# Layer 1 of a two-layer graph kernel: from group by group to batches of four groups

## The reference

```python
h = (x @ W).reshape(n, NHEAD, OUT_FEATS)            # 4 heads of 64
h_l = (a_l * h).sum(-1); h_r = (a_r * h).sum(-1)
e = h_l[row] + h_r[col]
e = jnp.where(e > 0, e, ALPHA * e)
m = jax.ops.segment_max(e, row, num_segments=n)
ex = jnp.exp(e - m[row])
denom = jax.ops.segment_sum(ex, row, num_segments=n)
att = ex / (denom[row] + 1e-16)
out = jax.ops.segment_sum(att[:, :, None] * h[col], row, num_segments=n)
```

## Time and profile before

| | us |
|---|---|
| median of 3 runs (lowest, highest) | 2514.63 (2512.04, 2518.51) |
| the profiled execution | 2514.38 |
| its span in the profile | 2512.6 |
| busy PE, DVE, ACT, POOL | 2155.4, 1961.2, 1689.9, 1587.8 |

### The profile page before, as it was taken

How to read it: one execution, slowest core, us unless ns; L and a number is a source line. 1 busy time by engine, 2 the same in 40 slices (tenths; PEclk the granted TensorE clock), 3 DMA queues, 4 the chain that set the end, 5 groups by cost and what they waited for, 6 DMA issues and landing times.

```text
span 2512.6 us, 62086 instructions
## 1 busy us (share of the span) xinstructions
PE 2155.4 (86%) x14858; PEld 1765.1 (70%) x14859; DVE 1961.2 (78%) x6401; ACT 1689.9 (67%) x6944; POOL 1587.8 (63%) x1700
## 2 busy tenths in 40 slices
PE   0579999999968888888888888869999999999994
PEld 0347777777747777777766776658888888888883
DVE  8983333333338999998989998879999999999998
ACT  2125555555547777777777775558888888888883
POOL 5346777777776565655555563157777777777772
PEclk9999999999989999999999999989999999999997
DMA  7243333333339999989989995123323222223232
GB/s 226 85 175 115 128 126 129 125 129 125 127 124 333 302 306 313 306 301 300 312 290 304 308 310 161 39 74 81 80 78 79 79 78 79 78 79 81 79 78 69
DMA packets 153328, 413.79 MB, mean 165 GB/s; under 512 B 40848, under 2 KB 53045, under 8 KB 153282
## 3 DMA queue, kind: packets, MB, share of 16 engines
q0 software_dynamic: 79360, 301.93, 37.4%
q1 hardware_dynamic: 73922, 111.33, 13.7%
HBM read 328.69 MB, written 84.60 MB: 164 GB/s over the span
## 4 chain that ended last, share of the span: by engine, by line
DVE 36%; issue 20%; DMA 18%; PE 12%; ACT 9%; DVEq 4%; POOL 1%; ACTq 0%; SPq 0%; POOLq 0%
DMA sorted_edges<-arena,idxA 8%; DMA arena<-sorted_edges 8%; DVE gmax L1111 6%; PE ps L1250 4%; ACT arena L617 3%; DVE arena L973 3%; DVE work L1130 2%; ACT arena L608 2%; DVE el L1106 2%; DVE hrmax L1119 2%; DVE sc L987 2%; DVE arena L980 2%; DVE gmax L1083 2%; PE ps L1283 2%; DVEq L286 1%
## 5 line engine op out<-in xcount | busy, mean ns | idle before, releaser
L548 POOL DMA_INDIRECT arena<-node_row,idxB x464 | 454.5, 980 | 209.2 <-issue 103.6
L474 POOL DMA_INDIRECT sorted_edges<-arena,idxA x416 | 410.4, 987 | 148.3 <-issue 147.4
L1361 PE MATMUL ps<-ident_b,arena 128*128 128x128 bf16 x5568 | 390.4, 220 | 53.0 <-DVE gmax L1111 26.8
L944 DVE TENSOR_TENSOR arena<-ps,b_bc 128x512 f32<-128x512 f32 x208 | 143.8, 691 | 354.6 <-PE ps L1250 354.6
L1250 PE MATMUL ps<-w_sb,arena 128*128 128x256 f32 x1664 | 386.9, 386 | 22.1 <-ACT arena L608 18.2
L1361 PEld LDWEIGHTS ps<-ident_b,arena 128*128 128x128 bf16 x5568 | 331.4, 100 | 87.8 <-DVE gmax L1111 31.4
L1250 PEld LDWEIGHTS ps<-w_sb,arena 128*128 128x128 f32 x1664 | 308.3, 190 | 99.8 <-issue 56.2
L494 POOL DMA_INDIRECT work<-node_kvx,idxB x232 | 234.3, 1010 | 165.1 <-issue 52.4
L494 POOL DMA_INDIRECT arena<-node_kvx,idxB x232 | 233.1, 1005 | 166.4 <-issue 53.0
L626 ACT ACTIVATE away<-iota,srcB 128x128 f32<-128x128 f32 x928 | 315.0, 386 | 0.2
L1283 PE MATMUL ps<-arena,work 128*128 128x256 f32 x928 | 252.9, 396 | 58.1 <-issue 52.1
(11 more groups left out here) (168 smaller groups left out, 4909.2 us busy)
## 6 DMA issues: line engine op xcount, KB each, us to landing
arena<-sorted_edges SPq DMA_DIRECT2D x232, 260.0 KB, 5.1
arena<-in_edge_attr SPq DMA_DIRECT2D x25, 512.0 KB, 3.6
node_kvx<-arena SPq DMA_DIRECT2D x24, 384.0 KB, 2.3
arena<-node_row,idxB POOLq DMA_INDIRECT x464, 2.8
sorted_edges<-arena,idxA POOLq DMA_INDIRECT x416, 2.4
sorted_edges<-arena SPq DMA_DIRECT2D x25, 260.0 KB, 2.1
sorted_edges<-arena SPq DMA_DIRECT2D x1, 6240.0 KB, 21.1
arena<-node_kvx,idxB POOLq DMA_INDIRECT x232, 5.2
```

The source lines that it names most:

```text
L474: pool.indirect_dma_start(rec_dram[:, :], bass.IndirectOffsetOnAxis(ap=idxA[:, st.slot(4), c:c + 1], axis=0), recA[:, st.slot(4), c, :], N ...
L548: pool.indirect_dma_start(row1_g[:, st.slot(8), j, :], None, row1_dram[:, :], bass.IndirectOffsetOnAxis(ap=idxB[:, st.slot(8), j:j + 1], a ...
L1361: pe.matmul(bank[:, h * P:(h + 1) * P], parts[:, i:i + 1].to_broadcast([P, P]), ident_b[:, :], start=h == 0 and part == 0, stop=False)
```

## The change

Four consecutive groups make a batch (BG = 4, 58 batches), and the loop is unrolled by 16.

- Spreading h_r: the 12 parts of both chunks are transposed by two matmuls with 12 stationary columns (`trh`), ACT copies them to SBUF (`hrT`), and for each head one matmul of 256 columns with a selector of 12 rows (`sel`) adds the three parts up on every row. The penalty is added by two matmuls of 512 columns. A group's four heads fill two banks, and a second pair of banks is for the next group.
- DVE takes one maximum over 256 numbers for each of 4 heads (1024 per row), the running maxima of a batch by one scan and three small steps backward, so that all groups of a tile in one batch share their maximum, and one rescaling of the running sums per batch in place of ACT's four per group.
- h_l, maxima, e and e - m are handled for the 8 chunks of a batch at once. The exponential is one of 32 numbers.
- DVE multiplies the messages of both chunks; POOL only gathers, and the gathered rows have 16 slots.
- The sums of a group have one PSUM bank, not two.

```diff
+    BG = 4
+    NB = NG // BG
+    ME = BG + 2
+    PARTS = 3 * NH1
...
 def gather1(st):
-    (POOL's product for chunk 1, L536)
+    if st.u % BG == 0:
+        pool.wait_ge(s("idxC_ready"), batch(st).n + 1)
+    if not st.first(16):
+        pool.wait_ge(s("msg1_ready"), st.n - 15)
...
 ACT, layer1(st):
+    g, b = st.u % BG, batch(st)
+    if g == 0:
+        f = b.back(-2)
+        if f.real():
+            indices(f)
+        e = b.back(2)
+        if e.real():
+            r = e.slot(2)
+            act.wait_ge(s("em"), e.n + 1)
+            ...
+            act.activation(ew[:, r, :, :], em[:, r, :, :], ACT.Exp).then_inc(s("exp1"), 1)
+            act.wait_ge(s("mdiff"), e.n + 1)
+            ...
+            act.activation(mscale[:, r, :], mdiff[:, r, :], ACT.Exp).then_inc(s("mscale"), 1)
+    if st.u % 8 == 0:
+        act_tiles[0] = tiles16(ACT_ENGINE, st.k, 0, st.u // 8)
+    if st.real():
+        (hl copy, two aways, one-hot)
+    c = st.back(1)
+    if c.real():
+        (pen, onehT8, hrT)
...
 DVE, layer1(st):
+    c = st.back(8)
+    if c.real():
+        (at the first group of a batch: rescale acc, wait for it)
+        dve.wait_ge(s("agg1_ready"), c.n + 1)
+        dve.tensor_tensor(acc, acc, ps[:, 5, 0:NH1 * HE], ALU.add)
+    if st.real():
+        dve.wait_ge(s("hr_mm"), st.n + 1)
+        dve.reduce_max(gmx[:, b.slot(2), :, 2 + g],
+                       ps[:, bank:bank + 2, :].rearrange("p c (h e) -> p (c h) e", h=2), axis=AX.X)
+    e = b.back(1)
+    if g == 1 and e.real():
+        (ez, el, es, em of 32, each waits for the one before)
+    m = st.back(6)
+    if m.real():
+        (at the first group of a batch: wait for exp1 of the batch)
+        (msg1 of both chunks, 520 per row)
+    if g == BG - 1 and st.real():
+        top(b, st)
...
+def top(b, last):   # each step waits for the one before
+    step(dve.tensor_tensor_scan(mfw, fresh, gmx, -BIG, ALU.add, ALU.max))
+    step(dve.tensor_copy(gmx[:, 1 - r, :, 0], mfw[:, :, ME - 1]))
+    for e in range(ME - 2, 1, -1):
+        step(dve.scalar_tensor_tensor(mfw[:, :, e], mfw[:, :, e + 1], fresh[...], mfw[:, :, e], ALU.add, ALU.max))
+    step(dve.tensor_tensor(zz, mfw[:, :, 1:ME], hmx[:, r, 0, :, :], ALU.add))
+    step(dve.scalar_tensor_tensor(hmx[:, r, 1, :, :], zz, SLOPE, zz, ALU.mult, ALU.max))
+    dve.sem_inc(s("hm_ready"), 1)
+    dve.tensor_tensor(mdiff[:, r, :], hmx[:, r, 1, 0, :], hmx[:, r, 1, 1, :], ALU.subtract)
...
 PE, layer1(st):
+    if st.real():
+        pe.wait_ge(s("oneh1"), n + 1)
+        transposes(r, oneh1[:, r16, 0, :], oneh1[:, r16, 1, :], s("oneh_tr1"))
+        pe.wait_ge(rows_in(r16), rows_base(r16) + 32 * st.turn(16) + 32)
+        (two matmuls into trh)
+    b = st.back(2)
+    if b.real():
+        (penalty 512 and two heads of 256, twice, waits gmax of two groups before)
+    e = batch(b).back(1)
+    if b.u % BG == 0 and e.real():
+        pe.wait_ge(s("onehT1"), BG * e.n + BG)
+        pe.wait_ge(s("hm_ready"), e.n + 1)
+        (8 matmuls, onehT8 stationary, 8 columns each)
+    d = st.back(9)
+    if d.real():
+        pe.wait_ge(s("msg1_ready"), n + 1)
+        pe.wait_ge(s("acc1_done"), n)
+        (two matmuls that sum the messages)
```

More of the change, by code:

```diff
@@ L33 @@
 BIG = 2.0 ** 100
+NEW = 2.0 ** 110
+FAR = 2.0 ** 120
 SLOPE = 0.2
@@ L289, in tiles_of, with tiles16, rows_in, rows_base @@
             return values
+        def tiles16(eng, k, lag, half):
+            _, values = nc.values_load_multi_w_load_instructions(
+                gt_i[0:1, bass.ds(k * 16 + (8 - lag + 8 * half), 8)], engines=(eng,), min_val=0, max_val=NT - 1,
+                skip_runtime_bounds_check_because="the table's values are bounded by the minimum with NT - 1")
+            return values
+        def rows_in(r):
+            if r < 8:
+                return s(f"kvx_in{r}")
+            return s(f"scattered{r - 8}") if r < 12 else s(f"row1_in{r - 12}")
+        def rows_base(r):
+            if r < 8:
+                return 32 * (NG // 8)
+            return 16 * 4 * (QUADS // 4) if r < 12 else 0
+        def batch(st):
+            return Step(st.k, st.u // BG, 16 // BG, NB)
         def heads_of(rows, st):
@@ L1142, in layer1 @@
-                if a.real():
-                    dve.wait_ge(s("hm_ready"), na + 1)
-                    dve.tensor_tensor(mdiff[:, a.slot(8), :], tile(mrun, ta), m_a, ALU.subtract).then_inc(
-                        s("mdiff"), 1)
-            run(dve, NG, 8, 8, layer1)
+                    dve.wait_ge(s("es"), e.n + 1)
+                    if not e.first(2):
+                        dve.wait_ge(s("exp1"), e.n - 1)
+                    dve.tensor_scalar(em[:, r, :, :], es[:, :, :], 0.0, None, ALU.min).then_inc(s("em"), 1)
@@ new lines, in layer1 @@
+                    pe.wait_ge(s("pen"), n + 1)
+                    pe.wait_ge(s("hrT"), n + 1)
+                    if not b.first(2):
+                        pe.wait_ge(s("gmax"), n - 1)
+                    for half in range(2):
+                        pe.matmul(ps[:, bank + half, :].rearrange("p (h e) -> p h e", h=2), ident_b[:, :],
+                                  pen[:, r4, :].unsqueeze(1).to_broadcast([P, 2, GJ * P]), start=True, stop=False)
+                        for h in range(2):
+                            ins = pe.matmul(ps[:, bank + half, h * GJ * P:(h + 1) * GJ * P],
+                                            sel[0:PARTS, 2 * half + h, :], hrT[0:PARTS, r4, :],
+                                            start=False, stop=h == 1)
```

353 lines of the change are left out of this document (171 added, 182 removed).

## The result

| us | before | after |
|---|---|---|
| median of 4 runs (lowest, highest) | 2513.34 (2509.59, 2518.51) | 3020.84 (3012.43, 3043.23) |
| the profiled execution | 2514.38 | 3015.41 |
| its span | 2512.6 | 3013.6 |
| mean granted clock | 0.971 | 0.802 |
| busy PE, DVE, ACT, POOL | 2155.4, 1961.2, 1689.9, 1587.8 | 2543.4, 1853.3, 1484.9, 1420.7 |

The changed kernel is slower: ratio 1.2028, 95% interval 1.1987 to 1.2070. The direction was forecast, the size was not: +508 us where +107 were expected, and 3021 lies far outside 2530 to 2745.

What follows compares the result with a forecast made beforehand. With PE and DVE nearly full before, a loop of waits through ACT, PE and DVE was to bound the changed kernel: 2512.6 + 78 + 4 + 25 (clock) = 2619.6 us of span, forecast 2621, range 2530 to 2745.

Steps and rivals of the forecast that it cites:

- a loop of waits: Layer 1, from `em` to `em` through ACT, PE and DVE: 15.3 us a batch against 13.98 before, +78 us.
- the clock's term: PE in layer 1: pauses put every third batch half at the low clock, 1.5 us each; +29, taken as 25 us.
- Steps 1, 4 and 6: Loop: ACT's exponentials to one-hot, 1.9 us; DVE's `top` until `hm_ready`, 1.96; DVE's maximum and steps on e, 1.9.
- Step 2: Loop, PE: transposes 0.22, parts 0.11, spreading 0.88, and 0.14 until the last lands; 1.35 us a batch.
- Step 3: Loop, DVE: maximum and messages, addition, the next group's maximum and messages; 3.8 us a batch.
- Step 5: Loop, PE: small matmuls 1.76, sum of messages 0.88, then the next transposes, parts and spreading 1.35; 4.0 us a batch.
- the rival: PE's clock low in most batches, half of 5.35 us each: 145 us on top of 2596, 2741; chance 0.12.
- a slower PE leaves fewer pauses: PE's clock in layer 1: reason given for taking 25 us where every third batch gave +29.
- The sign that I had named for that case: Profile after, layer 1: a granted clock under 0.85 would show the case of the low clock in most batches.
- The faster rival: ACT's exponential at the batch head does not hold PE; DVE's 3.0 to 3.1 us a group decide: 2420 us, chance 0.11.
- The relief from POOL's product: DVE no longer held by POOL's product, 0.44 us a group less 0.27 added: gain 39 us, 2475; chance 0.03.
- the end of layer 1 grows with the lag: Filling and draining layer 1's longer lag, 8 groups as before but in fours: +3 us (0 to 10).

Runs made afterwards that it cites:

- e2: Changed kernel with ACT's two exponentials moved behind the first step's one-hot, `pen`, `onehT8` and `hrT`: 2883.46 us, 1.0361 of the kernel before (changed kernel 1.1492 there).
- e8: Changed kernel in its own order with unread PE matmuls before the waits for the one-hot and for `hm_ready`: 2779.50 us, 1.1035 of the kernel before.
- e1: Changed kernel with selector matmuls over 128 rows, those beyond 12 zeros: 3051.55 us, 1.0971 of the kernel before (changed kernel 1.1492 there).
- e3: Changed kernel with both 128-row selectors and ACT's exponentials behind the one-hot: 2870.40 us, 1.0323 of the kernel before.
- e5: e3 with sums a group later, before the small matmuls, rescaling and addition after the maximum, exponentials ending the second step: 0.9877 of the kernel before; repeated elsewhere, 1.0036.
- run 16: Not a follow-up run: the words stand in "The gathers run 16 groups ahead", where "run" is a verb; no time or ratio belongs to it.
- e4: Changed kernel with 24 unread PE matmuls of 128 columns before the one-hot wait, once a batch: 3088.21 us, 1.1106 of the kernel before.
- e7: e5 with five unread PE matmuls of 512 columns before the wait for `hm_ready`: 2465.39 us, 0.9808 of the kernel before.

## Why the prediction was wrong

The direction came from the right mechanism, a loop of waits that is longer than any engine's work (e2 opens it and takes back 11 of 15 points). The step that failed is the clock's term, 25 us, and beside it the length of the loop, 15.3 us, was too short. Without the clock the forecast was 2596, so 3020.84 - 2596 = 425 us are to be explained. Two fillers alone, in the same order, gave back 241 of them (e8). As an estimate for the whole: a turn is 22.6 us in the profile after and 17.4 at the full clock in e8, so the low clock cost 58 x 5.2 = 302 us where 25 stood, and the longer loop 58 x (17.4 - 15.3) = 122, 424 together. The two are not quite apart, since e8's full-clock turns still hold its added matmuls; each share may be off by some ten us.

The loop, step by step, us a batch, from the two turns shown, both with the table's reading:

| step, as predicted | predicted | e8, full clock | after, clock 0.65 |
|---|---|---|---|
| 1. ACT, `em` to the one-hot | 1.9 | 2.35 | 2.46 |
| 2. PE, transposes, parts, spreading | 1.35 | 1.93 | 3.14 |
| 3. to the start of `top` | 3.8 | 4.58 | 5.73 |
| 4. `top` | 1.96 | 2.13 | 2.14 |
| 5. to the maximum of group 4B+5 | 4.0 | 4.85 | 7.57 |
| 6. maximum and steps on e | 1.9 | 2.00 | 2.08 |
| sum | 14.9 | 17.8 | 23.1 |

- Steps 1, 4 and 6 were right within 0.6 us (step 1 had the table at half, since only every second batch reads it). They are ACT's and DVE's, they don't change with PE's clock, and the durations from the earlier trace rows carried over; the scan took 0.20 us, as one of the small steps.
- Step 2, the spreading at 4 x 0.22 = 0.88, was too low: 4 x 0.32 = 1.28 at the full clock, since the spacing of 0.22 was read from weights of 128 rows and applied to weights of 12. e1 shows it. It enters the loop in steps 2, 3 and 5, 0.4 us each. Transposes and parts together took 0.52 to 0.58 from start to start where 0.33 stood, three times as well.
- Step 3 was put on DVE (max, product, addition, max, product). With a longer spreading PE's own way is later: sum 1.07, transposes and parts 0.43, spreading 1.3, then the maximum.
- Step 5 was short by the spreading's 0.4, 0.2 for transposes and parts, and 0.1 each for the small matmuls and the sum. It also had a wait that I left out: the sum waits for `acc1_done`, since the sums have one bank now, and the addition that sets it stands, on DVE, behind `top`, the reading of the table (in every second batch) and the rescaling. I had counted the table and the rescaling in DVE's busy time and left them out of the loop. In this order they cost almost nothing, 0.6 us in 650 in the profile after and 4.2 in e8, because the small matmuls take as long. Only where the loop is open does PE wait for the addition, 27.8 us in 600 in e3. e5 moves this piece, together with two others, and gains 4.5 points (1.0323 to 0.9877, different chips of the same kind).
- The clock was the largest error. I took half of PE's 5.35 us at the low clock in every third batch. No row gave the third, and the 1.5 us for such a batch was too low by my own numbers: half of 5.35 at half the clock is 2.7 more, as the rival had with 2.5. And 5.35 was not all of PE's part, as step 3 is PE's too: 1.93 + 2.82 + 4.85 = 9.6 us of the turn of e8 (2.82 until the maximum that begins at 2142.76), 3.14 + 3.98 + 7.57 = 14.7 of that after. In the profile after the clock is 0.61 over the 650 us: three of the five short windows stand at 0.50, and in two of them PE is busy for 4.00 of 4.00 us. PE's idle time is 650 - 572.72 = 77 us in these 650, 2.7 us a batch where I had expected 5, the longest wait for the one-hot 3.3 us; the low clock came back with each batch all the same, and PE stayed low while it worked on afterwards. More of its work in the batch pays than half of one part, and the loop grows by it, 17.8 to 23.1. The argument "a slower PE leaves fewer pauses" was half right: they are fewer, 2.7 us for 5, but the clock did not stay up, since DVE and ACT wait for PE and then PE for them again. The upper bound that I wrote down, 310 us, is about what it cost (302), by luck, as it counted 5.35 us of PE's part and not all; I chose 25, and gave the case in which it is low in most batches 0.12. The sign that I had named for that case, a clock under 0.85, came with 0.61, and even its 2741 was 280 us short. The rows for more were there: the earlier trace rows had 0.57 after one pause.
- The Trainium skill's TensorE: Matmul & The Clock Gate, section "Why this matters for your kernels", warns that idle gaps between bursts of matmuls put the clock back to half. The trace agrees with it (0.61 in layer 1, 0.94 once both pauses are filled), and the rival should have had the larger chance, as its mechanism was the right one.
- The faster rival needed a loop that doesn't bind; it does, and ACT's 274.9 us of waiting show it. The relief from POOL's product came as expected, a small step now takes 0.18 us where L1122 had taken 0.60, and it was worth nothing, as DVE had time to spare:

```profile
L1201 DVE TENSOR_SCALAR em<-es 128x32 f32<-128x32 f32 x28 | 5.1, 180 | 1.6
```

- The prediction gave the sentence of the Trainium skill's GPSIMD Engine Reference, section "Specifications", only in part: it names VectorE's two-port instructions too, beside those with two SBUF inputs. So the 0.60 us of L1122, with one input, does not show more than that rule, as the prediction had it; whether L1122 is such an instruction the trace does not say.
- That the end of layer 1 grows with the lag was estimated at +3. The gathers run 16 groups ahead, so from the last one to the end of the span there are 104.1 us after and 52.7 before. That is no cost of its own, only the last turns of the loop at their pace.

What stays open: why the clock rose by as much as 0.62 to 0.77 with the 128-row selectors, which shorten the loop but fill no pause (whether the number of rows matters to the clock by itself no run tests). And each of e5's three moves was not tried alone.

## What to carry to other kernels

When work is put into batches, write down for each engine what stands behind its first wait, and follow the circle through all engines with every wait in it, including those for buffers that the change has made fewer: its length, not the busiest engine, is the time. A pause of PE that recurs in every turn of such a circle can cost the clock in most of the work between the pauses, as here; then the price of all PE's work at the low clock is a likely case and not a bound. If work without a use in the pause makes the kernel faster, as in e4, e7 and e8, the clock was the cost. And a chain of waits tells which wait ended last, not how much is gained without it: look at how long the engine stood there.

## What the runs showed of the hardware that was not expected

- In these runs weight loads do not show between matmuls as long as the number of rows stays 128 (0.22 us from start to start for 512 columns), and do where it changes between 12 and 128 (0.32 us). At the low clock it is 0.54 (2111.39 after 2110.85 in the timeline of after) against 0.42 to 0.43 in e1. Zeros up to 128 rows were faster than the smaller matrix.
- Sixteen small fp32 matmuls (eight calls) took 1.85 us in e8 and 2.39 at 2104.47 in the profile after, where the clock was 0.72.
- Some chips take 2779 to 2791 us for the kernel before and others 2515, with nearly the same clock (0.950 and 0.971 over the span). Of the 274 us, 157 lie ahead of layer 1 and 117 in it, where the trace shows stops of ACT, DVE and POOL that end with "remote".
